# The two 128-column products of each attention head: three products of halves in place of one in plain float32

## The chip, the cores and the metric

The kernel runs on one core of a Trainium2 chip, as one program. The metric is the device time of the whole program in microseconds (us). A core has a matrix engine (PE in the profile; its weight loads are shown apart as PEld), a vector engine (DVE), a scalar engine (ACT), GpSimd (POOL) and SyncE (SP), each with its own stream of instructions; they wait for each other only through semaphores.

## The reference

One layer of a language model tower on 4 sequences of 512 tokens with 1024 features, all in float32: an embedding, causal attention with 32 query heads in 8 groups that share a key and a value head, and a small per-head feed-forward part.

```
h = tok(x)                                    # gather of rows, bias, position
h = h + attn(layernorm(h))                    # below
h = h + ffn(layernorm(h))                     # 16 heads of 64, 256 wide, gelu

def attn(q, w_qkv, w_dense):                  # 8 groups x 4 heads, head size 128
    qkv = q @ w_qkv.T
    scores = einsum('bskgd,btkd->bkgst', qh, kh) / sqrt(128)
    scores = where(causal, scores, lowest)
    attn = einsum('bkgst,btkd->bskgd', softmax(scores), vh)
    return attn @ w_dense.T
```

## The kernel before, in words

**Halves.** Nearly all products run on tiles of the type `F32R`, a rounded float32. A value x is kept as two such tiles, `hi` (x rounded, written by an ACT copy) and `lo` (x - hi, written by a DVE subtraction). `product` (lines 549 to 552) forms a*b as three matmuls into one PSUM bank: hi*hi (L550), hi*lo (L551), lo*hi (L552). Each loads 128 x 128 weights and streams the columns of the other operand, 512 in the projections.

**Tiles of a head.** A sequence of 512 is cut into 4 tiles of 128 (`TT`). For each of the 128 heads (4 sequences x 8 groups x 4 heads) PE does a step `S`, the scores: for query tile t the keys 0 to 128(t+1), so 128, 256, 384 and 512 columns, written to the bank `sc`. After the softmax, steps `Ta` and `Tb` turn the ten probability tiles (L585) into the bank `tp`, from where ACT and DVE split them into `pt_hi` and `pt_lo`. Step `PV`, the values: key tile j against queries 128j to 512, so 512, 384, 256 and 128 columns, into the bank `pv`.

**The two narrow products.** The products with 128 columns are the exception: the first query tile's scores (L576) and the last key tile's values (L599) are one matmul each on plain float32 tiles `q_first`, `k_first`, `v_last`, `pt_last`, which ACT copies out of PSUM by instructions of their own (L836, L833, L847, L823). The rest of Q, of the probabilities and of V is split from column 128 on, or up to the last tile, so those ACT copies and DVE subtractions are 384 or 128 columns wide (L837, L822, L846, L972, L957, L992).

**Order.** The order of the work is written out by hand in the strings `FIRST`, `MID`, `MLP` and others (lines 54 to 74); `schedule` turns them into one list of steps that all engines walk through. `D` is the output projection of the group before, `Q`, `K`, `V` the projections of the next group, `VT` turns V (L680), `U` and `O` are the feed-forward part of the sequence before (L637, L646). The weights of the projections are read from memory already split by SP's queue, 11 tiles ahead of their use; only in the first sequence ACT and POOL split them.

Of the kernel before, what the change touches and what calls it, by code (L numbers as in the profile page):

```python
# [6 lines left out]
F32 = mybir.dt.float32  # L7
F32R = mybir.dt.float32r
# [3 lines left out]
ALU = mybir.AluOpType  # L12
ACT = mybir.ActivationFunctionType

P = 128
B, S, E = 4, 512, 1024
G, HQ, D = 8, 4, 128
KT = E // P
TT = S // P
# [17 lines left out]

PT_OFF = [0, 512, 896]
PT_LEN = 1152

# [173 lines left out]
def tower_kernel(nc, x_cols, x_row, table, bias, pos, edge_cols, w_qkv, w_dense, w_mlp, perm_cols, out):  # L214
# [31 lines left out]
    with ctx:  # L246
        def sb(name, shape, dt, at=ctx):
            return at.enter_context(nc.sbuf_tensor(name, shape, dt))
# [20 lines left out]
        q_hi = sb("q_hi", [P, 2, S], F32R)  # L269
        q_lo = sb("q_lo", [P, 2, S], F32R)  # L270
        k_hi = sb("k_hi", [P, S], F32R)
        k_lo = sb("k_lo", [P, S], F32R)
        v_hi = sb("v_hi", [P, TT - 1, D], F32R)
        v_lo = sb("v_lo", [P, TT - 1, D], F32R)

# [4 lines left out]
        pt_hi = sb("pt_hi", [P, 2, PT_LEN], F32R)  # L280
        pt_lo = sb("pt_lo", [P, 2, PT_LEN], F32R)

        q_first = sb("q_first", [P, 2, P], F32)
        k_first = sb("k_first", [P, P], F32)
        pt_last = sb("pt_last", [P, 2, P], F32)
        v_last = sb("v_last", [P, D], F32)
        prob = sb("prob", [P, P_LEN], F32)
# [151 lines left out]
        def product_at(s):  # L439
            if s in ALONE:  # L440
                return first_bank(2 + ALONE.index(s))
            return pv[:, :] if aside(s) else fb[:, bank(s), :]
# [7 lines left out]
        def free(s):  # L450

            if s in ALONE:
                return (v_alone_free, 1) if s.kind == "V" else (alone_free, ALONE.index(s) + 1)
            if aside(s):
                return side_free, tally.side[s] + 1
            return bank_free[bank(s)], job[s] // 2 + 1
# [91 lines left out]
        def _(pe):  # L548
            def product(dst, a_hi, a_lo, b_hi, b_lo, first, last):
                pe.matmul(dst, a_hi, b_hi, start=first, stop=False)  # L550
                pe.matmul(dst, a_hi, b_lo, start=False, stop=False)  # L551
                return pe.matmul(dst, a_lo, b_hi, start=False, stop=last)  # L552
# [13 lines left out]
            def scores(s):  # L566
                q = s.i % 2
                pe.wait_ge(*free(Step("K", s.b, s.g, 0)))
                pe.wait_ge(*free(Step("Q", s.b, s.g, s.i)))
                if head(s) > 0:  # L570
                    pe.wait_ge(exp_done, 4 * head(s))
                else:
                    pe.wait_ge(last_free, 2)
                if tally.ups[s] > 0:
                    pe.wait_ge(g_done, tally.ups[s])
                pe.matmul(sc[:, 0, 0:P], q_first[:, q, :], k_first[:, :], start=True, stop=True)  # L576
                for t in range(1, TT):
                    at, c = SC_AT[t]
                    w = P * (t + 1)
                    qt = slice(t * P, (t + 1) * P)  # L580
                    product(sc[:, at, c:c + w], q_hi[:, q, qt], q_lo[:, q, qt],
                            k_hi[:, 0:w], k_lo[:, 0:w], True, True).then_inc(sc_full, 1)

# [3 lines left out]
            def values(s):  # L587
                r = s.i % 2

                pe.wait_ge(tpa_free, turn_a(Step("Tb", s.b, s.g, s.i)) + 1)  # L590
                if head(s) > 0:
                    pe.wait_ge(pv_free, head(s))
                if tally.sides[s] > 0:
                    pe.wait_ge(side_free, tally.sides[s])
                for j in range(TT - 1):
                    at = slice(PT_OFF[j], PT_OFF[j] + S - j * P)
                    product(pv[:, j * P:S], v_hi[:, j, :], v_lo[:, j, :], pt_hi[:, r, at], pt_lo[:, r, at],
                            j == 0, False)
                pe.matmul(pv[:, S - P:S], v_last[:, :], pt_last[:, r, :], start=False, stop=True).then_inc(pv_full, 1)  # L599

# [171 lines left out]
        def _(act):  # L772
# [35 lines left out]
            for s in STEPS:  # L808
# [8 lines left out]
                elif s.kind == "Ta":  # L817
# [3 lines left out]
                    act.wait_ge(tpb_full, turn_b(s) + 1)  # L821
                    act.activation(pt_hi[:, r, S:S + 384], tp[:, 1, 0:384], copy)  # L822
                    act.activation(pt_last[:, r, :], tp[:, 1, 384:S], copy).then_inc(tpb_hi, 1)  # L823
                elif s.kind == "Tb":
                    act.wait_ge(tpa_full, turn_a(s) + 1)
                    act.activation(pt_hi[:, s.i % 2, 896:PT_LEN], tp[:, 0, 0:256], copy).then_inc(tpa_hi, 1)
                elif s.kind == "PV":
                    act.wait_ge(pv_full, head(s) + 1)
                    act.activation(heads_of(s)[0][:, s.i, :], pv[:, :], copy).then_inc(at_rounded, 1)  # L829
                elif s.kind in ("Q", "K"):  # L830
                    act.wait_ge(*filled(s))
                    if s.kind == "K":
                        act.activation(k_first[:, :], product_at(s)[:, 0:P], copy)  # L833
                        act.activation(k_hi[:, :], product_at(s), copy).then_inc(split_hi, 1)
                    else:
                        act.activation(q_first[:, s.i % 2, :], product_at(s)[:, 0:P], copy)  # L836
                        act.activation(q_hi[:, s.i % 2, P:S], product_at(s)[:, P:S], copy).then_inc(split_hi, 1)  # L837
                elif s.kind == "V":
                    act.wait_ge(*filled(s))
                    act.activation(v_feat, product_at(s), copy).then_inc(free(s)[0], 1)  # L840
                elif s.kind == "VT":
# [3 lines left out]
                    act.wait_ge(tpb_full, turn_b(s) + 1)  # L845
                    act.activation(v_hi[:, 2, :], tp[:, 1, 0:D], copy)  # L846
                    act.activation(v_last[:, :], tp[:, 1, D:2 * D], copy).then_inc(tpb_hi, 1)  # L847
                elif s.kind == "H":
# [58 lines left out]
        def _(dve):  # L907
# [21 lines left out]
            for s in STEPS:  # L929
# [21 lines left out]
                elif s.kind == "Ta":  # L951
# [4 lines left out]
                    dve.wait_ge(tpb_hi, turn_b(s) + 1)  # L956
                    dve.tensor_tensor(pt_lo[:, r, S:896], tp[:, 1, 0:384], pt_hi[:, r, S:896], ALU.subtract)\  # L957
                       .then_inc(tpb_free, 1)
                elif s.kind == "Tb":
                    r = s.i % 2  # L960
                    dve.wait_ge(tpa_hi, turn_a(s) + 1)
                    dve.tensor_tensor(pt_lo[:, r, 896:PT_LEN], tp[:, 0, 0:256], pt_hi[:, r, 896:PT_LEN],
                                      ALU.subtract).then_inc(tpa_free, 1)
# [4 lines left out]
                elif s.kind in ("Q", "K"):  # L968
                    r, at = s.i % 2, slice(0 if s.kind == "K" else P, S)
                    hi, lo = (k_hi[:, at], k_lo[:, at]) if s.kind == "K" else (q_hi[:, r, at], q_lo[:, r, at])  # L970
                    dve.wait_ge(split_hi, tally.qk[s] + 1)
                    dve.tensor_tensor(lo, product_at(s)[:, at], hi, ALU.subtract).then_inc(free(s)[0], 1)  # L972
                    if s == Step("K", 0, 0, 0):
# [13 lines left out]
                elif s.kind == "VT":  # L987
# [3 lines left out]
                    dve.wait_ge(tpb_hi, turn_b(s) + 1)  # L991
                    dve.tensor_tensor(v_lo[:, 2, :], tp[:, 1, 0:D], v_hi[:, 2, :], ALU.subtract).then_inc(tpb_free, 1)  # L992
                elif s.kind == "D":
# [209 lines left out]
```

## Time and profile before

| | |
|---|---|
| median of 3 runs | 2640.26 us (2639.32 to 2641.65) |
| the profiled execution's own time | 2642.0 us |
| its span, first to last instruction | 2640.2 us |
| PE busy, matmuls | 2596.9 us, 98% of the span, 12970 |
| PEld busy, weight loads | 2113.9 us, 80%, 12970 |
| DVE busy | 1191.8 us, 45% |
| ACT busy | 983.5 us, 37% |
| POOL busy | 303.1 us, 11% |
| DMA | 428.82 MB, mean 162 GB/s |
| mean granted clock of TensorE | 0.996 of full speed |

The page shows one profiled execution; its own time lies 1.8 us above its span. Busy times of PE are those of records whose ends are modelled, and neighbouring records overlap, so what an instruction costs in a dense stretch is read from the distance between two starts and not from its mean length. A line of the timeline with "x2" merges two records; its start is that of the first. The trace prints `f32` for the halves and for plain float32 alike.

### The profile page before, as it was taken

The page shows a single profiled execution, that of the slowest core. Times are in us where ns is not written, and L with a number is a line of the kernel's source. Part 1 is how long each engine was busy: PE and PEld are TensorE (multiplying, and loading weights), DVE is VectorE, ACT ScalarE, POOL GpSimd, SP SyncE. Part 2 cuts the span into 40 slices and gives each one's busy share as a digit, 9 for nine tenths or more (in the row PEclk, how much of TensorE's full clock was granted, in tenths as well). Part 3 has the DMA queues.
Part 4 walks back from the last instruction along what each step waited for, and adds up shares of the span by engine and source line. Part 5 has one row for each costly group of instructions (what it writes and reads, how often), then busy time and mean ns, then how long its engine had stood idle before and what let it go on. Part 6 is the DMA issues. An engine that isn't in the chain of part 4 may idle for free.

```text
span 2640.2 us, 35093 instructions
## 1 busy us (share of the span) xinstructions
PE 2596.9 (98%) x12970; PEld 2113.9 (80%) x12970; DVE 1191.8 (45%) x3115; ACT 983.5 (37%) x2600; POOL 303.1 (11%) x254
## 2 busy tenths in 40 slices
PE   8999999999999999999999999999999999999997
PEld 6888888888877777888887877788888777778883
DVE  4444444554444344454444443445444344434444
ACT  4544444444243433324334333322423333332232
POOL 4233334332000000100000000010000000000002
PEclk9999999999999999999999999999999999999999
DMA  6466567654544334643343444363444444433432
GB/s 245 159 219 220 200 219 271 217 201 155 176 143 160 134 129 149 214 144 136 131 162 135 152 157 139 136 214 128 144 151 141 143 146 154 152 128 136 144 128 88
DMA packets 135190, 428.82 MB, mean 162 GB/s; under 512 B 15918, under 2 KB 15918, under 8 KB 135022
## 3 DMA queue, kind: packets, MB, share of 16 engines
q1 hardware_dynamic: 127488, 401.15, 43.1%
q0 software_dynamic: 7424, 25.17, 3.4%
q8 instruction: 105, 1.72, 0.3%
q14 instruction: 63, 0.52, 0.1%
q10 hardware_dynamic: 110, 0.26, 0.0%
HBM read 325.86 MB, written 100.66 MB: 162 GB/s over the span
## 4 chain that ended last, share of the span: by engine, by line
PE 95%; ACT 2%; DVE 1%; DMA 1%; issue 0%; POOL 0%; POOLq 0%; SPq 0%; ACTq 0%; DVEq 0%
PE fb L550 22%; PE fb L552 22%; PE fb L551 22%; PE tp L585 5%; PE sc L550 3%; PE sc L551 3%; PE sc L552 3%; PE pv L550 2%; PE sc L637 2%; PE pv L552 2%; PE pv L551 2%; PE fb L646 2%; PE sc L576 1%; PE pv L599 1%; PE fb L631 1%; PE tp L680 1%
## 5 line engine op out<-in xcount | busy, mean ns | idle before, releaser
L550 PE MATMUL fb<-xn_hi,w_both 128*128 128x512 f32 x1504 | 596.4, 397 | 1.1 <-DVE stats L1002 0.8
L552 PE MATMUL fb<-xn_hi,w_both 128*128 128x512 f32 x1504 | 587.5, 391 | 0.0
L551 PE MATMUL fb<-xn_lo,w_both 128*128 128x512 f32 x1504 | 586.2, 390 | 0.0
L550 PE MATMUL fb<-at_hi,w_both 128*128 128x512 f32 x992 | 394.2, 397 | 4.1 <-DVE hacc L997 3.8
L552 PE MATMUL fb<-at_hi,w_both 128*128 128x512 f32 x992 | 387.6, 391 | 0.0
L551 PE MATMUL fb<-at_lo,w_both 128*128 128x512 f32 x992 | 386.8, 390 | 0.0
L814 ACT ACTIVATE prob<-sc,neg_max 128x128 f32<-128x128 f32 (+3 forms) x512 | 263.0, 526 | 291.7 <-DVE neg_max L942 288.5
L550 PEld LDWEIGHTS fb<-xn_hi,w_both 128*128 128x128 f32 x1504 | 282.6, 188 | 77.0 <-issue 18.8
L997 DVE TENSOR_TENSOR hacc<-hacc,fb 128x512 f32<-128x512 f32 x256 | 175.9, 687 | 369.5 <-PE fb L552 369.3
L552 PEld LDWEIGHTS fb<-xn_hi,w_both 128*128 128x128 f32 x1504 | 282.4, 188 | 60.7
L551 PEld LDWEIGHTS fb<-xn_lo,w_both 128*128 128x128 f32 x1504 | 282.8, 188 | 57.1
L1099 POOL TENSOR_TENSOR w_both<-w_raw,w_both 128x512 fp32r<-128x512 f32 x168 | 215.1, 1297 | 423.6 <-ACT w_both L790 423.5
L939 DVE CUSTOM_DVE_ANT_0 sc<-sc,mask 128x128 f32<-128x128 f32 (+3 forms) x512 | 237.4, 519 | 2.4 <-PE sc L552 2.1
L550 PEld LDWEIGHTS fb<-at_hi,w_both 128*128 128x128 f32 x992 | 186.3, 188 | 52.7 <-issue 16.4
L967 DVE TENSOR_TENSOR at_lo<-pv,at_hi 128x512 fp32r<-128x512 f32 x124 | 85.6, 690 | 303.7 <-ACT at_hi L829 303.7
L552 PEld LDWEIGHTS fb<-at_hi,w_both 128*128 128x128 f32 x992 | 186.2, 188 | 39.9
L551 PEld LDWEIGHTS fb<-at_lo,w_both 128*128 128x128 f32 x992 | 186.5, 188 | 36.8
L972 DVE TENSOR_TENSOR q_lo<-fb,q_hi 128x384 fp32r<-128x384 f32 x126 | 70.3, 558 | 316.3 <-ACT q_hi L837 315.9
L585 PEld LDWEIGHTS tp<-ident,prob 128*128 128x128 f32 x1280 | 150.8, 140 | 53.1 <-issue 18.9
L585 PE MATMUL tp<-ident,prob 128*128 128x128 f32 x1280 | 183.8, 274 | 8.3 <-DVE pt_lo L954 7.8
L950 DVE TENSOR_SCALAR prob<-prob,inv_sum 128x128 f32<-128x128 f32 (+3 forms) x512 | 184.6, 425 | 4.5
L836 ACT ACTIVATE q_first<-fb 128x128 f32<-128x128 f32 x126 | 34.9, 277 | 389.1 <-PE fb L552 389.1
(198 smaller groups left out, 3461.4 us busy)
## 6 DMA issues: line engine op xcount, KB each, us to landing
w_both<-qkv_halves SPq DMA_DIRECT2D x280, 512.0 KB, 3.6
w_both<-dense_halves SPq DMA_DIRECT2D x192, 512.0 KB, 4.0
qkv_halves<-w_both SPq DMA_DIRECT2D x96, 512.0 KB, 3.9
dense_halves<-w_both SPq DMA_DIRECT2D x64, 512.0 KB, 3.3
w_raw<-in_w_qkv SPq DMA_DIRECT2D x104, 256.0 KB, 4.4
w_raw<-in_w_dense SPq DMA_DIRECT2D x64, 256.0 KB, 3.5
h_rows<-hacc SPq DMA_DIRECT2D x32, 256.0 KB, 2.2
h_tok<-in_pos SPq DMA_DIRECT2D x12, 512.0 KB, 6.0
```

Of the source, the lines that this page charges most:

```text
L550: pe.matmul(dst, a_hi, b_hi, start=first, stop=False)
L551: pe.matmul(dst, a_hi, b_lo, start=False, stop=False)
L552: return pe.matmul(dst, a_lo, b_hi, start=False, stop=last)
L585: return pe.transpose(tp[:, at, c:c + P], prob[:, P_OFF[t] + j * P:P_OFF[t] + (j + 1) * P], ident[:, :])
L637: pe.matmul(dst, weight[own, cols], rows[own, :], start=True, stop=True).then_inc(done, 1)
L814: act.activation(prob[:, P_OFF[t]:P_OFF[t] + w], sc[:, at, c:c + w], ACT.Exp, bias=neg_max[:, t:t + 1], scale=SCALE, accum_out=row_sum[:, ...
L939: dve.tensor_tensor_reduce(one, one, mask[:, S - w:S], 1.0, LOWEST, ALU.add, ALU.max, row_max[:, t:t + 1]).then_inc(tile_max, 1)
L950: dve.tensor_scalar(at, at, inv_sum[:, t:t + 1], None, ALU.mult).then_inc(prob_ready, 1)
L967: dve.tensor_tensor(lo[:, s.i, :], pv[:, :], hi[:, s.i, :], ALU.subtract).then_inc(pv_free, 1)
L972: dve.tensor_tensor(lo, product_at(s)[:, at], hi, ALU.subtract).then_inc(free(s)[0], 1)
L997: dve.tensor_tensor(hacc[:, s.i, :], hacc[:, s.i, :], fb[:, bank(s), :], ALU.add)\
L1099: pool.tensor_tensor(w_lo[:, m % RW, :], w_raw[:, raw[m] % RAW, :], w_hi[:, m % RW, :], ALU.subtract)\
```

## The change

The two narrow products are formed by `product` too. The tiles `q_first`, `k_first`, `pt_last` and `v_last` go; `v_hi`, `v_lo`, `pt_hi` and `pt_lo` get room for the fourth tile, and the splits of Q, of the probabilities and of V cover all columns with one ACT copy and one DVE subtraction. In step `S` the first product raises no semaphore of its own, as before. The lines of `product` are 545, 546 and 547 in the changed kernel.

```diff
-PT_OFF = [0, 512, 896]
-PT_LEN = 1152
+PT_OFF = [0, 512, 1024, 896]
+PT_LEN = 1280
...
-        v_hi = sb("v_hi", [P, TT - 1, D], F32R)
-        v_lo = sb("v_lo", [P, TT - 1, D], F32R)
+        v_hi = sb("v_hi", [P, TT, D], F32R)
+        v_lo = sb("v_lo", [P, TT, D], F32R)
...
-        q_first = sb("q_first", [P, 2, P], F32)
-        k_first = sb("k_first", [P, P], F32)
-        pt_last = sb("pt_last", [P, 2, P], F32)
-        v_last = sb("v_last", [P, D], F32)
...
-                pe.matmul(sc[:, 0, 0:P], q_first[:, q, :], k_first[:, :], start=True, stop=True)
-                for t in range(1, TT):
+                for t in range(TT):
                     at, c = SC_AT[t]
                     w = P * (t + 1)
                     qt = slice(t * P, (t + 1) * P)
-                    product(sc[:, at, c:c + w], q_hi[:, q, qt], q_lo[:, q, qt],
-                            k_hi[:, 0:w], k_lo[:, 0:w], True, True).then_inc(sc_full, 1)
+                    mm = product(sc[:, at, c:c + w], q_hi[:, q, qt], q_lo[:, q, qt],
+                                 k_hi[:, 0:w], k_lo[:, 0:w], True, True)
+
+                    if t > 0:
+                        mm.then_inc(sc_full, 1)
...
-                for j in range(TT - 1):
+                for j in range(TT):
                     at = slice(PT_OFF[j], PT_OFF[j] + S - j * P)
-                    product(pv[:, j * P:S], v_hi[:, j, :], v_lo[:, j, :], pt_hi[:, r, at], pt_lo[:, r, at],
-                            j == 0, False)
-                pe.matmul(pv[:, S - P:S], v_last[:, :], pt_last[:, r, :], start=False, stop=True).then_inc(pv_full, 1)
+                    mm = product(pv[:, j * P:S], v_hi[:, j, :], v_lo[:, j, :], pt_hi[:, r, at], pt_lo[:, r, at],
+                                 j == 0, j == TT - 1)
+                mm.then_inc(pv_full, 1)
...
-                    act.activation(pt_hi[:, r, S:S + 384], tp[:, 1, 0:384], copy)
-                    act.activation(pt_last[:, r, :], tp[:, 1, 384:S], copy).then_inc(tpb_hi, 1)
+                    act.activation(pt_hi[:, r, S:2 * S], tp[:, 1, :], copy).then_inc(tpb_hi, 1)
...
-                    if s.kind == "K":
-                        act.activation(k_first[:, :], product_at(s)[:, 0:P], copy)
-                        act.activation(k_hi[:, :], product_at(s), copy).then_inc(split_hi, 1)
-                    else:
-                        act.activation(q_first[:, s.i % 2, :], product_at(s)[:, 0:P], copy)
-                        act.activation(q_hi[:, s.i % 2, P:S], product_at(s)[:, P:S], copy).then_inc(split_hi, 1)
+                    hi = k_hi[:, :] if s.kind == "K" else q_hi[:, s.i % 2, :]
+                    act.activation(hi, product_at(s), copy).then_inc(split_hi, 1)
...
-                    act.activation(v_hi[:, 2, :], tp[:, 1, 0:D], copy)
-                    act.activation(v_last[:, :], tp[:, 1, D:2 * D], copy).then_inc(tpb_hi, 1)
+                    act.activation(v_hi[:, 2:4, :], tp[:, 1, 0:256].rearrange("p (j d) -> p j d", j=2), copy)\
+                       .then_inc(tpb_hi, 1)
...
-                    dve.tensor_tensor(pt_lo[:, r, S:896], tp[:, 1, 0:384], pt_hi[:, r, S:896], ALU.subtract)\
+                    dve.tensor_tensor(pt_lo[:, r, S:2 * S], tp[:, 1, :], pt_hi[:, r, S:2 * S], ALU.subtract)\
                        .then_inc(tpb_free, 1)
...
-                    r, at = s.i % 2, slice(0 if s.kind == "K" else P, S)
-                    hi, lo = (k_hi[:, at], k_lo[:, at]) if s.kind == "K" else (q_hi[:, r, at], q_lo[:, r, at])
+                    r = s.i % 2
+                    hi, lo = (k_hi[:, :], k_lo[:, :]) if s.kind == "K" else (q_hi[:, r, :], q_lo[:, r, :])
                     dve.wait_ge(split_hi, tally.qk[s] + 1)
-                    dve.tensor_tensor(lo, product_at(s)[:, at], hi, ALU.subtract).then_inc(free(s)[0], 1)
+                    dve.tensor_tensor(lo, product_at(s), hi, ALU.subtract).then_inc(free(s)[0], 1)
...
-                    dve.tensor_tensor(v_lo[:, 2, :], tp[:, 1, 0:D], v_hi[:, 2, :], ALU.subtract).then_inc(tpb_free, 1)
+                    dve.tensor_tensor(v_lo[:, 2:4, :], tp[:, 1, 0:256].rearrange("p (j d) -> p j d", j=2),
+                                      v_hi[:, 2:4, :], ALU.subtract).then_inc(tpb_free, 1)
```

On PE, at the seam where the values of a group's last head (`PV`) are followed by the turning of V (`tp<-ident,prob`) and the scores of the next group's first head, stands before:

```order
L552 MATMUL pv<-pt_hi,v_lo 128x256
L599 MATMUL pv<-pt_last,v_last 128x128
L680 MATMUL tp<-ident,prob 128x128 [waits tpb_free,tpa_free,bank0_free]
L680 MATMUL tp<-ident,prob 128x128 x3
L576 MATMUL sc<-k_first,q_first 128x128 [waits exp_done,g_done,bank0_free]
L550 MATMUL sc<-k_hi,q_hi 128x256
L551 MATMUL sc<-k_lo,q_hi 128x256
```

In these rows L599 and L576 are the two narrow products, one matmul each. At the same seam of the changed kernel stands:

```order
L547 MATMUL pv<-pt_hi,v_lo 128x256
L545 MATMUL pv<-pt_hi,v_hi 128x128
L546 MATMUL pv<-pt_lo,v_hi 128x128
L547 MATMUL pv<-pt_hi,v_lo 128x128
L677 MATMUL tp<-ident,prob 128x128 [waits tpb_free,tpa_free,bank0_free]
L677 MATMUL tp<-ident,prob 128x128 x3
L545 MATMUL sc<-k_hi,q_hi 128x128 [waits exp_done,g_done,bank0_free]
L546 MATMUL sc<-k_lo,q_hi 128x128
L547 MATMUL sc<-k_hi,q_lo 128x128
L545 MATMUL sc<-k_hi,q_hi 128x256
L546 MATMUL sc<-k_lo,q_hi 128x256
```

The one plain matmul of each place has become three matmuls on halves, 128 columns each; the semaphores waited for are the same and stand at the first of them. Over the program PE has 512 more matmuls in this listing, 2 for each of the 256 places.

## Rows read from the trace of the kernel before

**Rows 1.** Busy time of each engine, share of the span, instructions (the page, part 1)
```profile
PE 2596.9 (98%) x12970; PEld 2113.9 (80%) x12970; DVE 1191.8 (45%) x3115; ACT 983.5 (37%) x2600; POOL 303.1 (11%) x254
```

**Rows 2.** The chain of waits, shares of the span by engine (the page, part 4)
```profile
PE 95%; ACT 2%; DVE 1%; DMA 1%; issue 0%; POOL 0%; POOLq 0%; SPq 0%; ACTq 0%; DVEq 0%
```

**Rows 3.** A stretch: length, busy us of PE, PEld, DVE, ACT, POOL; PEclk, DMA
```profile
735.00:1400.00 665.00, 661.00 (x3304) 537.59 (x3303) 297.80 (x797) 236.88 (x634) 24.08 (x22) 1.00 0.44 150
```

**Rows 4.** Waits of PE: who waited for whom, total us, times, longest us
```profile
PE tp L585 <- DVE pt_lo L954: 7.8, 16, 1.4
PE fb L550 <- DVE hacc L997: 3.9, 10, 0.4
```

**Rows 5.** Groups by line and shape: count | busy us, mean ns | idle before
```profile
L576 PE MATMUL sc<-k_first,q_first 128*128 128x128 f32 x256 | 49.5, 275 | 0.0
L599 PE MATMUL pv<-pt_last,v_last 128*128 128x128 f32 x256 | 49.0, 273 | 0.0
L576 PEld LDWEIGHTS sc<-k_first,q_first 128*128 128x128 f32 x256 | 38.5, 190 | 0.0
```

**Rows 6.** Timeline of PE around a seam between two groups: start us, us, instruction
```profile
1214.96 0.29 PE L552 MATMUL pv<-pt_hi,v_lo 128*128 128x256 f32 x1
1215.09 0.38 PE L599 MATMUL pv<-pt_last,v_last 128*128 128x128 f32 x2
1215.30 0.60 PE L680 MATMUL tp<-ident,prob 128*128 128x128 f32 x4
1215.74 0.39 PE L576 MATMUL sc<-k_first,q_first 128*128 128x128 f32 x2
1215.88 0.36 PE L550 MATMUL sc<-k_hi,q_hi 128*128 128x256 f32 x1
1216.09 0.28 PE L551 MATMUL sc<-k_lo,q_hi 128*128 128x256 f32 x1
1216.20 0.28 PE L552 MATMUL sc<-k_hi,q_lo 128*128 128x256 f32 x1
1216.32 0.34 PE L550 MATMUL sc<-k_hi,q_hi 128*128 128x384 f32 x1
1216.49 0.34 PE L551 MATMUL sc<-k_lo,q_hi 128*128 128x384 f32 x1
1216.67 0.33 PE L552 MATMUL sc<-k_hi,q_lo 128*128 128x384 f32 x1
1216.84 0.39 PE L550 MATMUL sc<-k_hi,q_hi 128*128 128x512 f32 x1
1217.07 0.40 PE L551 MATMUL sc<-k_lo,q_hi 128*128 128x512 f32 x1
```

**Rows 7.** Timeline of the weight loads in the same stretch
```profile
1215.86 0.19 PEld L550 LDWEIGHTS sc<-k_hi,q_hi 128*128 128x128 f32 x1
1215.97 0.19 PEld L551 LDWEIGHTS sc<-k_lo,q_hi 128*128 128x128 f32 x1
1216.09 0.19 PEld L552 LDWEIGHTS sc<-k_hi,q_lo 128*128 128x128 f32 x1
```

**Rows 8.** Groups by shape: weight loads of 64 columns, and of the transposes
```profile
L585 PEld LDWEIGHTS tp<-ident,prob 128*128 128x128 f32 x1280 | 150.8, 140 | 53.1 <-issue 18.9 <-DVE pt_lo L954 11.1 <-DVE prob L950 0.3
...
L646 PEld LDWEIGHTS fb<-g,mlp_w 128*64 128x64 f32 x192 | 11.6, 136 | 19.4 <-issue 17.9
```

**Rows 9.** Groups by shape: copies by ACT and differences by DVE
```profile
L820 ACT ACTIVATE pt_hi<-tp 128x512 fp32r<-128x512 f32 x128 | 76.6, 599 | 132.0 <-PE tp L585 131.7
...
L972 DVE TENSOR_TENSOR q_lo<-fb,q_hi 128x384 fp32r<-128x384 f32 x126 | 70.3, 558 | 316.3 <-ACT q_hi L837 315.9
...
L837 ACT ACTIVATE q_hi<-fb 128x384 fp32r<-128x384 f32 x126 | 61.3, 486 | 0.0
...
L836 ACT ACTIVATE q_first<-fb 128x128 f32<-128x128 f32 x126 | 34.9, 277 | 389.1 <-PE fb L552 389.1
...
L972 DVE TENSOR_TENSOR k_lo<-fb,k_hi 128x512 fp32r<-128x512 f32 x31 | 21.4, 691 | 98.5 <-ACT k_hi L834 98.5
```

More of the change, by code:

```diff
@@ L821, in _ @@
                     act.wait_ge(tpb_full, turn_b(s) + 1)
-                    act.activation(pt_hi[:, r, S:S + 384], tp[:, 1, 0:384], copy)
-                    act.activation(pt_last[:, r, :], tp[:, 1, 384:S], copy).then_inc(tpb_hi, 1)
+                    act.activation(pt_hi[:, r, S:2 * S], tp[:, 1, :], copy).then_inc(tpb_hi, 1)
                 elif s.kind == "Tb":
                     act.wait_ge(tpa_full, turn_a(s) + 1)
-                    act.activation(pt_hi[:, s.i % 2, 896:PT_LEN], tp[:, 0, 0:256], copy).then_inc(tpa_hi, 1)
+                    act.activation(pt_hi[:, s.i % 2, 2 * S:PT_LEN], tp[:, 0, 0:256], copy).then_inc(tpa_hi, 1)
                 elif s.kind == "PV":
@@ L961, in _ @@
                     dve.wait_ge(tpa_hi, turn_a(s) + 1)
-                    dve.tensor_tensor(pt_lo[:, r, 896:PT_LEN], tp[:, 0, 0:256], pt_hi[:, r, 896:PT_LEN],
+                    dve.tensor_tensor(pt_lo[:, r, 2 * S:PT_LEN], tp[:, 0, 0:256], pt_hi[:, r, 2 * S:PT_LEN],
                                       ALU.subtract).then_inc(tpa_free, 1)
```

## The prediction

> **What bounds the kernel now.** I read the page's busy times first. PE is busy for 98% of the span; the next engine, DVE, for 45% [rows 1]. A busy PE is not yet a PE at its limit, so the chain of waits came second: 95% of the chain that ended last runs over PE, ACT has 2%, DVE and DMA 1% each [rows 2]. Third, a long stretch in the middle: PE covers 661.0 of 665.0 us at a granted clock of 1.00, the upper level, 2.4 GHz, while DVE, ACT and DMA have more than half of it free [rows 3]. Last, PE's own waits: the two largest come to 7.8 us in 16 waits and 3.9 us in 10 [rows 4]. So the program is a queue of matmuls in dense order. A nanosecond that a step adds on PE is added to the end almost wholly, and work taken from ACT or DVE brings next to nothing. The question is what one narrow product costs on PE before and what three cost after.
>
> **What the narrow products cost now.** Each plain float32 matmul shows as two records on PE and two weight loads: 256 records for the 128 heads, of 275 and 273 ns [rows 5]. Those lengths overlap with their neighbours, so I take distances between starts [rows 6]. Values: from the first L599 record at 1215.09 to the next instruction, L680, at 1215.30 are 0.21 us. Scores: from L576 at 1215.74 to the second product of the next trio, L551 at 1216.09, are 0.35 us, in which lie the two plain records and one L550 with 256 columns. Products with 256 columns start 0.11, 0.12 and, at 1214.96 to 1215.09, 0.13 apart (1216.09, 1216.20, 1216.32); I take one at 0.117 and have 0.233 left. Together 0.443 us per head, 56.7 us for 128 heads. That is the whole of what goes on PE.
>
> **What comes.** Six products of halves with 128 columns per head, 768 in all. The kernel before has no product of halves so narrow, so the cost X of one is bounded from both sides.
>
> The low bound is the streaming of the columns. In rows 6 products of 256, 384 and 512 columns start 0.117, 0.175 and 0.23 us after one another, about 0.057 for 128 columns more. If nothing but columns counted, X would be 0.06 us: 6 x 0.06 = 0.36, 0.083 less than the 0.443 of now.
>
> The high bound is the plain product of the same shape, 0.22 us (half of 0.443), if a narrow product of halves ran at the pace of a plain one: 6 x 0.22 = 1.32, or 0.88 more per head.
>
> Between them lies the weight load. Each product loads 128 columns of weights, also where the weights are those of the product before (L550 and L551 both load q_hi). The loads start 0.11 and 0.12 us apart next to products of 256 columns [rows 7], and a load record is 190 ns long [rows 5], so part of it is latency that overlaps with the next load. How much is no latency can be read from the one form with half as many columns: 64 columns of weights take 136 ns [rows 8], 54 less than 190. So 128 columns take about 108 ns in which the load path is taken. A product of 256 columns or more hides this behind its own stream; one of 128 columns, with 0.06 us of stream, can't. On this reading a chain of narrow products goes at the pace of its loads: X is 0.108 at least and 0.117 if the handing over costs as much as it does between products of 256 columns. I take 0.117, the nearest row of the same kind of product. What speaks against it is the row of the transposes, whose loads of 128 columns last only 140 ns [rows 8]; but four of them in a row (L680) also stand 0.11 us apart (1215.30 to 1215.74) [rows 6], so no chain in these rows goes faster than that.
>
> On this the Trainium skill agrees with the row, and it speaks against the change: "TensorE: Matmul & The Clock Gate", section "LDWEIGHTS (loading the stationary operand)", gives a load the time of its columns over 1.2 GHz, an estimate of 107 ns for 128 columns whatever the matmul streams. By that figure alone the six products would be 0.64 us per head and the sum about 25 us above now. [...]
>
> **The sum.** PE per head: 6 x 0.117 = 0.702, less 0.443, is +0.259 us; for 128 heads +33.2 us. With X = 0.108 it would be +0.205 and +26.2 us.
>
> The cover that takes some of it: PE waits 16 times for DVE's L954, 7.8 us in all [rows 4], before a `Tb` step that mostly follows a `PV`. Where the values run 0.14 us longer (0.351 for 0.21), such a wait is shorter by as much: up to -2.2 us, and I take -1.5.
>
> ACT and DVE: per Q projection ACT had two copies of 277 and 486 ns and now has one of 512 columns, 599 by the row of the same width; DVE's difference grows from 558 to 691 ns, by the row for K [rows 9]. The pair is done 31 ns earlier (-164, +133). The same holds for K, `Ta` and `VT` in kind: an ACT instruction less, a wider DVE one. All of it lies beside PE's products, of which there are several us between a projection and the scores that use it; in the other direction, if every one of PE's 16 waits for DVE grew by that 0.13 us, it would be +2.1 us. I cost it at 0. SP and POOL issue what they did; a weight tile that is read later because PE is later has the DMA engines at 0.44 of their time [rows 3] and is due later too. The tail of the program (feed-forward of the last sequence) has no such product.
>
> So +33.2 - 1.5 = +31.7 us against the profiled execution's own 2642.0 us (span 2640.2 and 1.8 around it): 2673.7. The median of the three runs is 1.7 below that execution, so I forecast 2672 us, 1.2% slower.
>
> **The rivals.**
>
> Stream-bound, faster. The loads run ahead of the products and only columns count: X = 0.06, -0.083 x 128 = -10.6 us, 2630 us. For it: PE's queue does start a load before the product in front of it has ended [rows 6, 7]. Against it: the 54 ns between loads of 64 and 128 columns [rows 8], and that transposes, 128 columns too, never stand nearer than 0.11. It decides if two loads can be in flight wholly side by side, that is if X comes below 0.074, where 6X is 0.443.
>
> Partly hidden loads, no or little change. The load path is shorter than its records say, X = 0.085 halfway between the bounds: 0.51 per head, +0.067 x 128 = +8.6 us, 2649 us. The section "Back-to-back issue gap" of the same page on TensorE gives about 81 ns per product of 128 columns in a stream of loads and matmuls, which would make +5 us; no row here shows such a distance.
>
> The pace of plain float32. A product of halves with 128 columns doesn't get the pace of the wide ones and takes what the plain one takes: X = 0.22, +0.88 x 128 = +112 us, 2753 us. For it: all narrow rows of the trace are of the slow kinds, so nothing shows a narrow product at one pass. Against it: distances fall evenly from 512 over 384 to 256 columns [rows 6] with no sign of a step.
>
> That the change does nothing to PE is excluded by the listing of its instructions: 512 matmuls more.
>
> **How the numbers follow.** Load-bound 0.74 (2672 us; with X from 0.108 to 0.14 and ACT and DVE at their bounds 2662 to 2690), partly hidden 0.08 (2649), stream-bound 0.09 (2630), pace of plain float32 0.09 (2753). A measurement of this kernel can tell 0.2%, 5.3 us, from no change. Faster by more than that: the stream-bound case, 0.09, and a little of the partly hidden one, 0.10. Within: what lies between 0.067 and 0.081 us for X, 0.03. Slower: the rest, 0.87. The range of 8 in 10 takes the load-bound case and the partly hidden one: 2645 to 2690; the other two are left out with 0.18.
>
> **What would show it.** Right: in the profile after, narrow products of halves start 0.11 to 0.12 us apart, their loads too; values' last trio takes about 0.35 us and scores' first trio the same; PE and PEld have 256 records more; PE's share stays at 98% and its waits don't grow. Wrong: starts 0.06 apart (stream-bound) or 0.2 and more apart, or one product shown as several records (plain pace); a wait of PE for `q_lo`, `k_lo` or `pt_lo` in the microseconds (the DVE term); or a granted clock below 1.00 in the middle stretch.

## The result and the profile after

The changed kernel takes 2663.76 us (median of 3 runs, 2661.48 to 2665.33) against 2640.26 us: 23.5 us more, ratio 1.0086, interval 1.0072 to 1.0100. Measured again later, beside other kernels, it takes 2663.59 us against 2640.79, ratio 1.0087 (1.0073 to 1.0101). The profiled execution is the fastest of the three, 2661.48 us at a span of 2659.6.

First the page's busy times and its chain by engine, to be laid beside [rows 1, 2].

```profile
PE 2616.7 (98%) x13226; PEld 2139.2 (80%) x13226; DVE 1233.1 (46%) x3115; ACT 961.7 (36%) x2280; POOL 303.7 (11%) x254
...
PE 95%; ACT 2%; DVE 2%; DMA 1%; issue 0%; POOL 0%; POOLq 0%; SPq 0%; ACTq 0%; DVEq 0%
```

PE has 256 records more, as two records per plain product became three per trio. Its share stays at 98% and its part of the chain at 95%. The stretch from 735 to 1400 us, beside [rows 3] (busy us of PE, PEld, DVE, ACT, POOL; granted clock; DMA):

```profile
735.00:1400.00 665.00, 660.87 (x3333) 539.05 (x3332) 306.15 (x791) 228.65 (x545) 24.06 (x22) 1.00 0.44 149
```

The clock is granted in full there, as before. PE's two largest waits, beside [rows 4]:

```profile
PE tp L582 <- DVE pt_lo L946: 7.0, 17, 1.3
PE fb L545 <- DVE hacc L990: 3.9, 10, 0.4
```

They are 0.8 us shorter in sum; all the waits that this view lists for PE come to 33.7 us, against 33.6 before. So the time went neither into waits nor into the clock; it went into PE's own row of products. The same seam as in [rows 6], on PE's timeline (start us, length us, instruction):

```profile
1224.27 0.29 PE L547 MATMUL pv<-pt_hi,v_lo 128*128 128x256 f32 x1
1224.39 0.22 PE L545 MATMUL pv<-pt_hi,v_hi 128*128 128x128 f32 x1
1224.45 0.28 PE L546 MATMUL pv<-pt_lo,v_hi 128*128 128x128 f32 x1
1224.56 0.28 PE L547 MATMUL pv<-pt_hi,v_lo 128*128 128x128 f32 x1
1224.67 0.62 PE L677 MATMUL tp<-ident,prob 128*128 128x128 f32 x4
1225.05 0.30 PE L545 MATMUL sc<-k_hi,q_hi 128*128 128x128 f32 x1
1225.19 0.28 PE L546 MATMUL sc<-k_lo,q_hi 128*128 128x128 f32 x1
1225.31 0.27 PE L547 MATMUL sc<-k_hi,q_lo 128*128 128x128 f32 x1
1225.42 0.33 PE L545 MATMUL sc<-k_hi,q_hi 128*128 128x256 f32 x1
1225.59 0.28 PE L546 MATMUL sc<-k_lo,q_hi 128*128 128x256 f32 x1
1225.71 0.28 PE L547 MATMUL sc<-k_hi,q_lo 128*128 128x256 f32 x1
1225.83 0.34 PE L545 MATMUL sc<-k_hi,q_hi 128*128 128x384 f32 x1
1226.00 0.34 PE L546 MATMUL sc<-k_lo,q_hi 128*128 128x384 f32 x1
1226.18 0.33 PE L547 MATMUL sc<-k_hi,q_lo 128*128 128x384 f32 x1
1226.35 0.39 PE L545 MATMUL sc<-k_hi,q_hi 128*128 128x512 f32 x1
```

From the last 256-column product of the values to the first 512-column one of the scores it is 1226.35 - 1224.27 = 2.08 us; before, in [rows 6], 1216.84 - 1214.96 = 1.88. That is 0.20 us more for one head. Inside, the narrow products of the scores start 0.14, 0.12 and 0.11 us apart. The first distance of the values (1224.39 to 1224.45) is only 0.06, the time of the columns alone, while the loads below start 0.11 apart at the same place. A single start can stand early; the sum over a trio, or the loads, tell the pace. The weight loads of that stretch, beside [rows 7]:

```profile
1224.39 0.19 PEld L546 LDWEIGHTS pv<-pt_lo,v_hi 128*128 128x128 f32 x1
1224.50 0.19 PEld L547 LDWEIGHTS pv<-pt_hi,v_lo 128*128 128x128 f32 x1
1224.64 0.42 PEld L677 LDWEIGHTS tp<-ident,prob 128*128 128x128 f32 x4
1225.03 0.19 PEld L545 LDWEIGHTS sc<-k_hi,q_hi 128*128 128x128 f32 x1
1225.14 0.19 PEld L546 LDWEIGHTS sc<-k_lo,q_hi 128*128 128x128 f32 x1
1225.25 0.19 PEld L547 LDWEIGHTS sc<-k_hi,q_lo 128*128 128x128 f32 x1
1225.36 0.19 PEld L545 LDWEIGHTS sc<-k_hi,q_hi 128*128 128x128 f32 x1
1225.47 0.19 PEld L546 LDWEIGHTS sc<-k_lo,q_hi 128*128 128x128 f32 x1
```

Between 1224.39 and 1224.50, and from 1225.03 to 1225.47, loads start 0.11 us apart, one after another, whatever the products beside them stream. PE goes at the pace of its weight loads here.

The copy and the subtraction of Q, beside [rows 9]:

```profile
L964 DVE TENSOR_TENSOR q_lo<-fb,q_hi 128x512 fp32r<-128x512 f32 x126 | 87.1, 691 | 309.5 <-ACT q_hi L829 309.5
...
L829 ACT ACTIVATE q_hi<-fb 128x512 fp32r<-128x512 f32 x126 | 75.3, 598 | 395.7 <-PE fb L547 395.7
```

One copy of 598 ns in place of 277 + 486, and a subtraction of 691 for 558, as expected. PE waits for this subtraction six times, 1.2 us together, which the kernel before doesn't show:

```profile
PE fb L720 <- DVE q_lo L964: 0.6, 3, 0.2
PE fb L545 <- DVE q_lo L964: 0.6, 3, 0.2
```

### The profile page after: what moved, and what is told of

Its sections match the earlier page's. It is cut to its first block, busy times and chain, and to the rows that moved or that the text cites. A ratio compares the mean times of both kernels' runs of the same rounds, so it can differ in the third digit from the quotient of the medians.

```text
span 2659.6 us, 35285 instructions
## 1 busy us (share of the span) xinstructions
PE 2616.7 (98%) x13226; PEld 2139.2 (80%) x13226; DVE 1233.1 (46%) x3115; ACT 961.7 (36%) x2280; POOL 303.7 (11%) x254
## 4 chain that ended last, share of the span: by engine, by line
PE 95%; ACT 2%; DVE 2%; DMA 1%; issue 0%; POOL 0%; POOLq 0%; SPq 0%; ACTq 0%; DVEq 0%
PE fb L545 22%; PE fb L547 22%; PE fb L546 22%; PE tp L582 5%; PE sc L546 3%; PE sc L547 3%; PE sc L545 3%; PE pv L546 3%; PE pv L547 3%; PE pv L545 3%; PE sc L634 2%; PE fb L643 2%; PE fb L628 1%; PE tp L677 1%; ACT w_both L787 1%
## 5 line engine op out<-in xcount | busy, mean ns | idle before, releaser
L964 DVE TENSOR_TENSOR q_lo<-fb,q_hi 128x512 fp32r<-128x512 f32 x126 | 87.1, 691 | 309.5 <-ACT q_hi L829 309.5
L829 ACT ACTIVATE q_hi<-fb 128x512 fp32r<-128x512 f32 x126 | 75.3, 598 | 395.7 <-PE fb L547 395.7
```

What stands on the lines that cost most here:

```text
L829: act.activation(hi, product_at(s), copy).then_inc(split_hi, 1)
L964: dve.tensor_tensor(lo, product_at(s), hi, ALU.subtract).then_inc(free(s)[0], 1)
```

## Experiments

Each was timed in 5 rounds beside the kernel before. Two theories of where the 23.5 us come from were set against each other. *Loads*: in a narrow product the load of the next weights, 0.11 us, outlasts the stream, 0.06, and a load runs only one product ahead. *Columns and a surcharge*: a narrow product costs its stream, and the place as a whole pays something fixed, for the change of form or for a wait.

**The two halves of the change apart.** Against the kernel before, the first run changes only the scores (the first two lines removed, one added), the second only the values (the rest):

```diff
-                pe.matmul(sc[:, 0, 0:P], q_first[:, q, :], k_first[:, :], start=True, stop=True)
-                for t in range(1, TT):
+                for t in range(TT):
...
-                for j in range(TT - 1):
+                for j in range(TT):
...
-                pe.matmul(pv[:, S - P:S], v_last[:, :], pt_last[:, r, :], start=False, stop=True).then_inc(pv_full, 1)
```

Scores alone: 

> Only the scores of the first query tile go to three products of halves; the values of the last key tile stay one plain product. Theory (loads): a narrow product of halves costs the load of the next weights, about 0.113 us, so the trio costs 0.337 for 0.224 us of the plain one: +0.113 us x 128 = +14.5 us over the kernel before, about 2655 us. Rival (the difference lies outside the narrow products, in the wider DVE subtractions or in later waits): the two halves of the change don't share the 23.5 us as 0.113 to 0.08, and PE's waits for DVE grow here by several us.

Measured: 2653.88 us against 2641.14, ratio 1.0048 (1.0034 to 1.0062), +12.7 us.

Values alone: 

> Only the values of the last key tile go to three products of halves; the scores stay as before. In the profile of the changed kernel the values' trio costs 0.087 us more where transposes follow, 0.095 where wide products follow, 0.061 where the feed-forward part follows. Theory (loads): +10.3 us less about 1 us that hides behind waits for DVE, so about 2649 to 2651 us, and together with the scores alone the whole +23.5 us. Rival (something that only both together bring): the two parts don't add up to the whole.

Measured: 2650.46 us against 2641.14, ratio 1.0036 (1.0023 to 1.0050), +9.3 us. The two add up to 22.1 us, within the intervals of the whole, 23.5. That is 0.100 us per head for the scores' trio and 0.073 for the values'; the intervals of the two runs overlap, so that the times alone don't tell one from the other. Each half alone carries its part, and they don't need each other.

**PE's part apart from that of ACT and DVE.** The changed kernel with one plain product in each narrow place:

```diff
-                for t in range(TT):
+                pe.matmul(sc[:, 0, 0:P], q_hi[:, q, 0:P].bitcast(F32), k_hi[:, 0:P].bitcast(F32), start=True, stop=True)
+                for t in range(1, TT):
...
+                pe.matmul(pv[:, S - P:S], v_hi[:, TT - 1, :].bitcast(F32), pt_hi[:, r, 896:2 * S].bitcast(F32),
+                          start=False, stop=True).then_inc(pv_full, 1)
```

> The changed kernel's copies and subtractions (full width, four fewer kinds of copy), but one plain float32 product in each of the 256 places, which reads the hi halves as float32; the lo part of these two products is left out. PE has the instructions of the kernel before, ACT and DVE those of the changed one. Theory (all of the cost is PE's): the time of the kernel before, 2640 us, within 0.1%. Rival (wider DVE subtractions cost, 133 ns each, or the saved ACT copies give something back): a few us above or below 2640 us.

Measured: 2639.19 us against 2641.14, ratio 0.9995 (0.9986 to 1.0004). Its busy times:

```profile
PE 2595.8 (98%) x12970; PEld 2113.4 (80%) x12970; DVE 1228.2 (47%) x3115; ACT 961.3 (36%) x2280; POOL 303.0 (11%) x254
```

DVE carries 36 us more than in [rows 1] and ACT 22 less, and the time is the same within its interval. The wider subtractions and the saved copies are worth between -0.14% and +0.04%, so all of the cost is PE's. (PE's six short waits for `q_lo` stand in this trace too, 1.2 us; they don't show in the time.)

**Twice the columns, the same loads.**

```diff
-                    w = P * (t + 1)
+                    w = max(P * (t + 1), 2 * P)
```

> The changed kernel, but the first query tile's scores are formed against 256 keys in place of 128 (the second 128 columns are overwritten by the next trio): twice the columns at the same number of weight loads. Theory (loads): a distance goes from 0.113 to the 0.117 or 0.12 of products with 256 columns, 3 x 0.005 x 128 = +2 us over the changed kernel, about 2666 us. Rival (columns are what a narrow product pays, on top of a fixed surcharge for the trio): 3 x 0.055 x 128 = +21 us, about 2685 us.

Measured: 2666.65 us against 2641.14, ratio 1.0100 (1.0084 to 1.0115), 3 us over the changed kernel. (The second 128 columns lie in a part of the bank that nobody reads, and are not overwritten as the expectation has it.) On PE's timeline the first trio of the scores, from its second product, and the start of the next:

```profile
1225.82 0.28 PE L546 MATMUL sc<-k_lo,q_hi 128*128 128x256 f32 x1
1225.93 0.28 PE L547 MATMUL sc<-k_hi,q_lo 128*128 128x256 f32 x1
1226.05 0.28 PE L545 MATMUL sc<-k_hi,q_hi 128*128 128x256 f32 x1
1226.17 0.28 PE L546 MATMUL sc<-k_lo,q_hi 128*128 128x256 f32 x1
```

Products with 256 columns start 0.11 to 0.12 us apart, those with 128 in the changed kernel, from the second of a trio on, also 0.11 to 0.12. Twice the columns are streamed for 3 us where columns would have cost 21. The intervals of the two times overlap, but the medians over all 128 steps of the two timelines say the same: 0.025 us more per step. This is against the second theory: in these trios a second 128 columns are almost free.

**Half a load, the same columns.** The middle product of each narrow trio has 64 columns of weights:

```diff
+            def narrow(dst, a_hi, a_lo, b_hi, b_lo, first, last):
+                pe.matmul(dst, a_hi, b_hi, start=first, stop=False)
+                pe.matmul(dst[0:P // 2, :], a_hi[:, 0:P // 2], b_lo, start=False, stop=False)
+                return pe.matmul(dst, a_lo, b_hi, start=False, stop=last)
```

> The changed kernel, but the middle product of each narrow trio has 64 columns of weights in place of 128 (so the hi*lo part of half the outputs is left out): the same number of products and streamed columns, a load half as long. Theory (loads, one ahead): only the distance from the first to the second narrow product, in which the half load runs, shrinks, from 0.113 to about 0.06: 0.053 x 256 = -13.6 us against the changed kernel, about 2650 us. Rival (columns plus a surcharge for the trio): no change, 2664 us.

Measured: 2651.27 us against 2641.22, ratio 1.0038 (1.0024 to 1.0052), 12 to 13 us under the changed kernel for 13.6 expected. The trio of the scores on PE, and its weight loads:

```profile
1219.28 0.30 PE L550 MATMUL sc<-k_hi,q_hi 128*128 128x128 f32 x1
1219.42 0.22 PE L551 MATMUL sc<-k_lo,q_hi 128*64 128x128 f32 x1
1219.48 0.28 PE L552 MATMUL sc<-k_hi,q_lo 128*128 128x128 f32 x1
1219.59 0.33 PE L545 MATMUL sc<-k_hi,q_hi 128*128 128x256 f32 x1
```

```profile
1219.25 0.19 PEld L550 LDWEIGHTS sc<-k_hi,q_hi 128*128 128x128 f32 x1
1219.36 0.14 PEld L551 LDWEIGHTS sc<-k_lo,q_hi 128*64 128x64 f32 x1
1219.42 0.19 PEld L552 LDWEIGHTS sc<-k_hi,q_lo 128*128 128x128 f32 x1
1219.53 0.19 PEld L545 LDWEIGHTS sc<-k_hi,q_hi 128*128 128x128 f32 x1
```

The load of 64 columns (`128*64`) is followed after 0.06 us by the next, one of 128 after 0.11; and the products follow the loads: 0.06 from the second to the third. The number of products and the columns that they stream are unchanged; the load is half as long (and half the outputs of that product are left out), and half of the whole cost went.

**Narrow between wide.** The three narrow products of the scores stand one by one behind the three with 512 columns:

```diff
+                for n in range(3):
+                    mm = piece(3, n)
+                    last = piece(0, n)
+                last.then_inc(sc_full, 2)
```

> The changed kernel, but the three narrow products of the scores stand one by one between the three with 512 columns, whose stream of 0.21 us is twice as long as a load; DVE takes the query tiles in the order 2, 1, 0, 3. Theory (loads, one ahead): a load can start only when the product before it has started, so behind each narrow product the next load is still in the open, and the time stays, 2664 us within 3 us. Rival (loads can run several products ahead and only a row of narrow ones drains them): each narrow product costs its 0.06 us of stream, 0.16 x 128 = -20 us, about 2643 us.

Measured: 2663.91 us against 2641.22, ratio 1.0089 (1.0075 to 1.0103): no change. The weight loads of these pairs (x2 is a wide and a narrow product's):

```profile
1226.65 0.36 PEld L585 LDWEIGHTS sc<-k_hi,q_hi 128*128 128x128 f32 x2
1227.05 0.30 PEld L585 LDWEIGHTS sc<-k_lo,q_hi 128*128 128x128 f32 x2
1227.39 0.30 PEld L585 LDWEIGHTS sc<-k_hi,q_lo 128*128 128x128 f32 x2
```

A pair takes 1227.39 - 1227.05 = 0.34 us, that is 0.23 for the wide product and 0.11 for the narrow one (the 0.40 before it are 0.17 of the last 384-column product and 0.23 of a wide one). The 0.21 us of stream of the wide one can't be used to load two products' weights. So a load runs one product ahead and no more, as far as this order tells, and a narrow product costs a load wherever it stands among products of halves.

**One product per place.** Only hi*hi is left in the two narrow places:

```diff
+            def narrow(dst, a_hi, a_lo, b_hi, b_lo, first, last):
+                return pe.matmul(dst, a_hi, b_hi, start=first, stop=last)
```

> The changed kernel, but each narrow place has the hi*hi product alone (hi*lo and lo*hi of the two narrow places are left out): the price of one and of two narrow products. Theory (loads): two loads of about 0.11 us less in each place: -0.225 us per scores and about -0.19 per values, -53 us against the changed kernel, about 2611 us, 29 us under the kernel before. Rival (columns plus a surcharge that the place pays once): 2 x 0.06 x 256 = -30 us, about 2634 us.

Measured: 2611.75 us against 2641.22, ratio 0.9888 (0.9873 to 0.9903), 52 us under the changed kernel. The theory of columns and a surcharge had 30 us here. Two narrow products less in 256 places are 512 products, 0.10 us each, against 0.06 for their columns. This also gives the exchange rate: a plain product costs about two narrow products of halves, which is why three lose and one would win; but one leaves out the low halves, and is no version of this kernel. The 0.10 is a little low, because PE waits longer here, for DVE above all (7.0 us in the changed kernel):

```profile
PE tp L585 <- DVE pt_lo L949: 10.8, 18, 1.8
```

All of PE's listed waits come to 38.6 us, 4.9 more than in the changed kernel; with these the 512 products are worth about 57 us, an estimate of 0.11 us each, the pace of the loads. Medians over the steps of the two timelines give the same: two products less are 0.22 us per step at the scores, and at the values 0.23 before transposes, 0.21 to 0.22 before wide products of a projection and 0.22 before feed-forward products. The starts at the values:

```profile
1203.33 0.29 PE L547 MATMUL pv<-pt_hi,v_lo 128*128 128x256 f32 x1
1203.46 0.22 PE L550 MATMUL pv<-pt_hi,v_hi 128*128 128x128 f32 x1
1203.52 0.62 PE L680 MATMUL tp<-ident,prob 128*128 128x128 f32 x4
```

The transposes seem to start 0.06 us after the narrow product; again the single distance is too short, and only the time of the whole and a sum over the group show the 0.11.

**Why the values' trio is the cheaper one against the plain product.** Medians over the 128 steps of the two timelines, taken between the same two wide or plain instructions around a trio, give the scores' trio 0.113 us more than the plain product; the values' trio 0.087 before transposes (61 steps), 0.095 before wide products (18) and 0.061 before feed-forward products (36). I supposed that the last distance of a trio is the load of the instruction that follows, and loads of transposes (140 ns for 190, [rows 8]) and of the feed-forward part hold the path for less.

```diff
-                for j in range(TT):
+                for j in (0, 3, 1, 2):
```

> The changed kernel, but the values' narrow trio stands second in its step, between the products with 512 and those with 384 columns, and not last. Theory (the third distance of a trio is the load of whatever follows): the values' trio costs less than the scores' because transposes (61 of 128 steps) or feed-forward products (36) follow it, whose loads hold the path for less time. Followed by a wide product of halves in all 128 steps it costs 0.03 us more before transposes and 0.057 more before feed-forward products: about +4 us against the changed kernel, 2668 us. Rival (the values' trio is cheaper because it adds onto a bank that is being filled, or because of its operands): no change, 2664 us.

The changed kernel as it is, beside it: 

> The changed kernel once more, beside the one with the other order, so that the two are compared on one chip. All theories: 2664 us, 0.9% above the kernel before.

Measured: 2663.20 us for the other order (ratio 1.0086, 1.0072 to 1.0100) and 2663.59 for the changed kernel (1.0087, 1.0073 to 1.0101). The trio in its new place on PE:

```profile
1222.55 0.22 PE L545 MATMUL pv<-pt_hi,v_hi 128*128 128x128 f32 x1
1222.61 0.28 PE L546 MATMUL pv<-pt_lo,v_hi 128*128 128x128 f32 x1
1222.72 0.27 PE L547 MATMUL pv<-pt_hi,v_lo 128*128 128x128 f32 x1
1222.83 0.39 PE L545 MATMUL pv<-pt_hi,v_hi 128*128 128x384 f32 x1
1223.06 0.33 PE L546 MATMUL pv<-pt_lo,v_hi 128*128 128x384 f32 x1
1223.23 0.34 PE L547 MATMUL pv<-pt_hi,v_lo 128*128 128x384 f32 x1
```

Down to the second 384-column product it takes 0.51 us (1222.55 to 1223.06), of which 0.17 or 0.18 are the wide one's, so 0.33 to 0.34 for the trio, three loads as in the scores. But the time didn't rise by the 4 us that I expected. The sizes don't allow a verdict: over the whole of both timelines the steps before feed-forward products are 0.045 us longer and those before transposes 0.010, which would be 2 us together, less than the intervals tell apart.

The run with one product per place narrows it down. The trio is 0.22 us above one narrow product of halves at the scores and 0.21 to 0.23 at the values, so the two products added cost the same in both. What differs is how far the plain product stood above one narrow product: in the same medians 0.11 us at the scores, at the values 0.12 before wide products, 0.14 before transposes and 0.16 before feed-forward products. Either the plain product was dearer in front of those, or the last product of halves is cheaper there; no run tells these two apart, and the cause stays open.

## Why the prediction was right, point by point

**The bound.** PE's row sets the end: 98% busy and 95% of the chain before and after, and the plain products put back on PE with all else left changed give the old time. Right, and shown.

**What goes.** 0.443 us per head for the two plain products was not measured by itself. If a trio counts 3 x 0.112 = 0.336 us in both places, the plain product of the scores was worth 0.336 - 0.113 = 0.22 us, near the 0.233 that was read, and that of the values before transposes 0.336 - 0.087 = 0.25, before feed-forward products 0.27, more than the 0.21 read from the seam. These are estimates, from medians of the traces.

**X, the price of a narrow product.** It was chosen as 0.117 us between 0.06 and 0.22, for the load. The mechanism was right: longer streams cost 3 us, shorter loads give 12 to 13 back, another order gives nothing. The size was a little high: for the scores +0.118 was forecast (0.351 less 0.233), the timelines show 0.113 and the run alone 0.100. The pace is nearer to 0.112, between the 0.108 worked out from the 64-column loads and the 0.117 taken over from products with 256 columns.

**The term that was mis-sized** is that of the values: three times 0.117 less 0.21, +0.141 us per head, of which the timelines show 0.061 to 0.095 and the run alone 0.073. One price for the narrow products of both places was right, as the run with one product shows; what was too small is the 0.21 for the plain product that goes, if the last product of halves isn't what is cheaper there. With 0.100 and 0.073 the sum is 22.1 us; with 0.259 per head it was 33.2. Of that miss of 0.086 us per head 0.068 lie in the values by the runs, 0.018 in the scores; a price X of 0.112 for 0.117 explains 0.015 in either place. That is why 2672 us was 8 us above the measured 2664, inside the range. The sign that the forecast named, a last trio of the values that takes about 0.35 us with starts 0.11 to 0.12 apart, was not seen as such: at the seam it takes 0.28 (1224.39 to 1224.67), with one distance of 0.06, a figure that the forecast had named as the sign of the stream-bound case. Its loads and the runs speak for the loads all the same.

**The cover.** -1.5 us was put on PE's waits for DVE before the transposes; these shrank by 0.8 us, and other waits of PE grew by as much (33.6 us in all before, 33.7 after, in one trace each). Nothing of the cover can be seen in the sum.

**ACT and DVE at 0.** Right in the time: 0.9995 with the changed copies alone, and the measured lengths are those taken from the rows of the same width. A small part of the cost that was put at nothing does show, PE's six waits for `q_lo`, 1.2 us.

**The bounds of the load-bound case.** They were given as 2662 and 2690 us. By the forecast's own terms X = 0.14 gives +50.8 us over the program, and with -1.5, +2.1 and the 2640.3 that it starts from it is 2692; X = 0.108 with -2.2 gives 2664. The measured time lies at that lower end.

**The rivals.** Stream-bound (2630 us) is refuted by the time, by the 0.11 between loads and by the doubled columns. Partly hidden loads (2649 us) would need X = 0.085, which neither a trio of the scores shows nor the 0.22 us for two products. The pace of plain float32 (2753 us) is refuted by one record per product and 0.11 us. On the Trainium skill: the section "LDWEIGHTS (loading the stationary operand)" of "TensorE: Matmul & The Clock Gate" gives a load the time of its columns over 1.2 GHz, an estimate of 107 ns for 128 columns, and the traces agree, 0.11 us for 128 and 0.06 for 64. The about 81 ns per product of 128 columns in its section "Back-to-back issue gap" were not met by these float32 halves, in no trio of the scores.

## What to carry to other kernels

In these runs a product on TensorE costs the longer of its own stream and the next product's weight load. For these rounded float32 tiles with 128 columns of weights the two meet near 256 streamed columns (0.117 us a product there, 0.112 at 128 columns), and below that width splitting one product into three is paid in loads, not in columns. So compare the number of weight loads, and not the streamed columns alone: a plain float32 product of 128 columns shows two, its three-product replacement three. And read a chain of short products from the starts of the loads or from a sum over the group, since single starts of short matmuls can stand 0.06 us apart where the chain moves at 0.11.

## What the runs showed of the hardware that was not expected

Wide products don't lend their spare stream time to short neighbours further off: with a 512-column product ahead of each narrow one, whose stream is twice a load, the pair still took 0.34 us and the program the same 2663.9 us. In a place of this kind twice as many streamed columns cost 0.008 us per product (3 us over 384 products). A plain product's price, too, depends on what follows it: against one narrow product of halves in its place it cost 0.11 us more at the scores and up to 0.16 more before feed-forward products, or the product of halves gains that there; the traces don't say which.
